# Attention on 128-pixel tiles: quarter matmuls for t, the out projection and the centring, and the q and k biases added by GpSimd

## The reference, cut to what matters

```python
xn = groupnorm(x)                       # 8 groups
t = xn @ ciw.T + cib + pe[image]        # "t"
tn = layernorm(t)
q2, k2, v2 = ((tn @ wq.T + bq) @ wiq.T + biq), ...   # q and k biases
attn = softmax(q2 . k2 / sqrt(8))       # over the 8 images, for each head
z = (attn @ v2) @ wout.T + bout         # out projection
t = z + t
tn2 = layernorm(t)                      # centring, then variance
m = (tn2 @ w1.T + b1) * gelu(t @ w2.T + b2) @ w3.T + b3
out = (m + t) @ cow.T + cob + x
```

## Time and profile before

| | us |
|---|---|
| median of 3 runs | 1245.43 |
| the profiled execution's own time | 1244.47 |
| its span, first to last instruction | 1242.5 |
| of it: before the first `pe_t` (setup) | 58.7 |
| first `pe_t` to the last `dve_x` of the attention | 627.0 |
| the rest: convolutions and the last stores | 556.8 |
| PE, DVE busy over the span | 1147.9, 1104.6 |
| ACT, POOL busy over the span | 648.7, 417.1 |

### The profile page before, as it was taken

One profiled execution on the slowest core, in us unless ns is written; L12 is line 12 of the kernel. 1 busy time (PEld: TensorE's weight loads), 2 busy tenths in 40 slices (PEclk: granted clock), 3 DMA queues, 4 the chain that ended last, 5 costly groups with the idle time before them and its releaser, 6 DMA issues. The chain is left out here.

```text
span 1242.5 us, 20220 instructions
## 1 busy us (share of the span) xinstructions
PE 1147.9 (92%) x6594; PEld 625.4 (50%) x6594; DVE 1104.6 (89%) x1521; ACT 648.7 (52%) x1518; POOL 417.1 (34%) x384
## 2 busy tenths in 40 slices
PE   3169999999999999999998899999999999999995
PEld 2156766766766776776763333333333333333331
DVE  4648999999999999999995799999999999999995
ACT  1356787787777777777763224233323422342422
POOL 3112313312322322322321344444444453455440
PEclk9989999999999999999999899999999999999998
DMA  8010111111101101101000000030001100030003
GB/s 300 18 33 18 33 29 27 35 27 29 30 25 34 25 25 34 25 25 35 18 13 14 1 1 1 1 63 5 1 1 29 40 2 1 1 68 1 1 1 68
DMA packets 87508, 35.34 MB, mean 28 GB/s; under 512 B 70209, under 2 KB 86850, under 8 KB 86930
## 3 DMA queue, kind: packets, MB, share of 16 engines
q1 hardware_dynamic: 85634, 33.81, 10.3%
q0 software_dynamic: 768, 0.33, 0.1%
q10 hardware_dynamic: 1040, 0.35, 0.1%
HBM read 26.09 MB, written 8.39 MB: 28 GB/s over the span
## 5 line engine op out<-in xcount | busy, mean ns | idle before, releaser
L1012 PE MATMUL acc<-mixed,cwp 128*128 128x512 f32 x768 | 354.8, 607 | 4.0 <-DVE mixed L1073 2.5
L1012 PEld LDWEIGHTS acc<-mixed,cwp 128*128 128x128 f32 x768 | 139.7, 191 | 217.8 <-issue 214.5
L1030 ACT ACTIVATE y<-acc,cols 128x1024 f32<-128x1024 f32 x96 | 111.8, 1210 | 249.2 <-PE acc L1022 249.2
L769 POOL TENSOR_TENSOR rstd<-var,half 128x8 f32<-128x8 f32 x32 | 80.2, 2507 | 382.0 <-DVE var L733 382.0
L1022 PE MATMUL acc<-mixed,cwp 64*64 64x512 f32 x1536 | 184.2, 600 | 11.4 <-POOL mixed L1073 11.4
L485 DVE TENSOR_TENSOR prod<-qkv 128x1024 f32<-128x1024 f32 x128 | 155.7, 1218 | 3.9 <-DVE qkv L675 1.5
L495 DVE TENSOR_TENSOR prod<-attn,qkv 128x1024 f32<-128x1024 f32 x128 | 153.2, 1216 | 0.0
L521 PE MATMUL b<-consts,prod 128*128 128x128 f32 x1024 | 139.1, 281 | 1.2 <-DVE prod L485 1.0
L1072 POOL TENSOR_TENSOR mixed<-xs 128x256 f32<-128x256 f32 x92 | 83.0, 902 | 156.7 <-DVE xs L1061 156.7
L1038 DVE TENSOR_TENSOR y<-y,acc 128x512 f32<-128x512 f32 x192 | 120.5, 679 | 15.6 <-ACT y L1030 15.6
L540 PE MATMUL b<-consts,prod 128*128 128x128 f32 x1024 | 128.8, 273 | 0.8 <-DVE var L733 0.3
(11 more groups left out here) (165 smaller groups left out, 1612.7 us busy)
## 6 DMA issues: line engine op xcount, KB each, us to landing
xs<-in_x SPq DMA_DIRECT2D x4, 2048.0 KB, 16.5
xa<-in_x SPq DMA_DIRECT2D x32, 256.0 KB, 2.7
xr<-in_x SPq DMA_DIRECT2D x64, 128.0 KB, 2.8
out_y<-xs SPq DMA_DIRECT2D x32, 256.0 KB, 4.7
cw<-in_L_conv_w POOLq DMA_DIRECT2D x2, 144.0 KB, 4.1
consts<-in_consts ACTq DMA_DIRECT2D x1, 192.0 KB
group<-in_consts SPq DMA_DIRECT2D x1, 64.0 KB
w1n<-in_L_conv_w ACTq DMA_DIRECT2D x1, 64.0 KB
```

The source lines that it names most:

```text
L1012: pe.matmul(psum[PSUM_PAIR[v, q, j]][i][:, :, :], weights(v, i, j).rearrange("p n o -> p (n o)"), mixed[v][i][:, s0:s0 + WIDE, j, :], star ...
L1030: act.activation(pairs(y[i][q][:, :, :]), m1, ACT.Identity, bias=cols[:, (6, 8)[v]:(7, 9)[v]]).then_inc(m1_out[i][q], 1)
```

## The change

- `pe_t`, `pe_z1`, `pe_center` and the `cowT` matmuls (now `pe_cow`) no longer use the block diagonal 128 x 128 matrix (or its halves in turn), but four quarter matmuls of 64 x 64, one for each quarter of the array, with half of the columns each: 8 of 128 columns for t, 4 of 256 for the out projection, 4 of 256 for the centring. The halves of the partitions now hold images 0 to 3 and 4 to 7, not the even and the odd. `pe_cow` is a step of its own behind `pe_scores_t` b = 2; its four matmuls were in two pairs.
- `pe_t` writes into `q_ps` rather than b2, and waits for `raw_out[1]`; `pe_qkv` g = 1 waits for `raw_out[0]`. `z1`, `cen2` and `sq2` are read from two banks, 256 columns of each.
- `pe_var2` takes 2 columns of `cmean` in place of 128.
- `dve_bias` becomes `pool_bias`: the same instruction on GpSimd.
- The order on all engines is written anew, over five tiles (t to t-4, 36 iterations), and no loop is left: all iterations are unrolled.

The diff, cut; of the order lists only the new ones stand. Semaphores were renamed and split to fit, and `dve_x`, `act_squares`, `act_raw` index images by d rather than e.

```diff
-            link(dve.tensor_tensor(top["tcol"][:, :], pt[0][:, 0:PAIRS], pet[:, :], ALU.add))
+            for e in range(2):
+                link(dve.tensor_tensor(top["tcol"][:, 2 * e:2 * e + 2], pt[e][:, 0:2], pet[:, 2 * e:2 * e + 2], ALU.add))
...
-                mm = pe.matmul(pt[0][half, 0:PAIRS], ciwT[half, :], gb[half, :], start=True, stop=True)
+                for k in range(2):
+                    mm = pe.matmul(pt[m][C * k:C * k + C, 0:2], ciwT[half, :], gb[half, 2 * k:2 * k + 2], start=True, stop=True)
...
-        gel = [sb(f"gel{e}", [P, N]) for e in range(2)]
-        gated = [sb(f"gated{e}", [P, N]) for e in range(2)]
+        gel = sb("gel", [P, 2 * N])
+        gated = sb("gated", [P, 2 * N])
...
+        cb = ctx.enter_context(nc.psum_tensor("cb", [P, 2, 512], F32))
+        zb = ctx.enter_context(nc.psum_tensor("zb", [P, 2, 512], F32))
...
+        b4, b2 = cb[:, 0, :], cb[:, 1, :]
+        b6, b3 = zb[:, 0, :], zb[:, 1, :]
+        HALF = N // 2
...
         def pe_t(pe, t, k):
             wait_loaded(pe, xa_in, t, k)
-            wait(pe, tn2_done, t - 3)
-            for p in range(PAIRS):
-                m = pe.matmul(b2[:, TILE * p:TILE * (p + 1)], top["resT"][:, p, :], xa[k % 2][:, p, :], start=True, stop=True)
+            wait(pe, raw_out[1], t)
+            for j in range(2):
+                for e in range(2):
+                    for d in range(2):
+                        m = pe.matmul(q_ps[half(d), e, 0, TILE * j:TILE * (j + 1)], top["resT"][half(e), 2 * d + j, half(e)],
+                                      xa[k % 2][half(e), 2 * d + j, :], start=True, stop=True)
             m.then_inc(t_mm, 1)
         def pe_qkv(pe, t, k, g):
             wait(pe, t_out, t + 1)
-            wait(pe, raw_out, 2 * t + g)
+            if g == 0:
+                wait(pe, t_out, t + 1)
+            else:
+                wait(pe, raw_out[0], t + 1)
...
         def pe_scores_t(pe, t, b):
             if b == 0:
-                wait(pe, t_out, upto(t + 2))
+                wait(pe, sq2_out, t - 1)
+                wait(pe, cen2_out, t - 1)
...
         def pe_z1(pe, t):
             wait(pe, z_out, t + 1)
+            wait(pe, shift_done, upto(t + 2))
             wait(pe, gelu_out[0], t)
-            pe.matmul(b6[:, :], top["woutT"][:, :], z[:, :], start=True, stop=True).then_inc(z1_mm, 1)
+            for e in range(2):
+                for d in range(2):
+                    m = pe.matmul(zb[half(d), e, 0:HALF], top["woutT"][half(e), half(e)],
+                                  z[half(e), HALF * d:HALF * (d + 1)], start=True, stop=True)
+            m.then_inc(z1_mm, 1)
         def pe_center(pe, t, k):
             wait(pe, z1_out, t + 1)
+            wait(pe, tn2_done, t)
             wait(pe, z_out, t + 1)
-            pe.matmul(b4[:, :], center, z1[k % 2][:, :], start=True, stop=True).then_inc(cen2_mm, 1)
+            for d in range(2):
+                for e in range(2):
+                    m = pe.matmul(cb[half(e), d, 0:HALF], center[half(d), half(d)],
+                                  z1[k % 2][half(d), HALF * e:HALF * (e + 1)], start=True, stop=True)
+            m.then_inc(cen2_mm, 1)
...
-                m = pe.matmul(b4[:, P * p:P * (p + 1)], sq2[:, TILE * p:TILE * (p + 1)], cmean, start=True, stop=True)
+                m = pe.matmul(b4[:, 2 * p:2 * p + 2], sq2[:, TILE * p:TILE * (p + 1)], cmean[:, ::C], start=True, stop=True)
...
+        def pe_out(pe, t, d):
+            for e in range(2):
+                wait(pe, gated_done[e], t + 1)
             for r in range(2):
-                pe.matmul(out_of(e, r), top["w3T"][:, :], rows(gated[e][:, :], r), start=True, stop=False)
-            for r in range(2):
-                m = pe.matmul(out_of(e, r), top["cowT"][half, :], rows(z1[k % 2][half, :], r), start=False, stop=True)
-            m.then_inc(out_mm[e], 1)
+                m = pe.matmul(out_of(d, r), top["w3T"][:, :], rows(gated[:, N * d:N * (d + 1)], r), start=True, stop=False)
+            m.then_inc(out_mm[d], 1)
+
+        def pe_cow(pe, t, k):
+            for d in range(2):
+                for r in range(2):
+                    m = pe.matmul(out_of(d, r), top["cowT"][half(d), :], rows(z1[k % 2][half(d), :], r), start=False, stop=True)
+            m.then_inc(cow_mm, 1)
...
+            for e in range(2):
+                for j in range(2):
+                    blk = 2 * e + j
+                    m = act.activation(tt[k][:, TILE * blk:TILE * (blk + 1)], q_ps[:, e, 0, TILE * j:TILE * (j + 1)],
+                                       ACT.Identity, bias=top["tcol"][:, blk:blk + 1])
...
-        def dve_bias(dve, t, k):
-            wait(dve, scaled_out, B * (t + 1))
+        def pool_bias(pool, t, k):
+            wait(pool, scaled_out, B * (t + 1))
             qk = qkv[k][:, :, 0:2 * C]
-            dve.tensor_tensor(qk, qk, top["brep"][:, :].unsqueeze(1).broadcast_to([P, B, 2 * C]), ALU.add).then_inc(biased, 1)
+            pool.tensor_tensor(qk, qk, top["brep"][:, :].unsqueeze(1).broadcast_to([P, B, 2 * C]), ALU.add).then_inc(biased, 1)
...
-            for e in range(2):
-                wait(dve, out_mm[e], t - 1)
-            dve.scalar_tensor_tensor(z1[k % 2][:, :], b6[:, :], cols[:, 1:2], tt[k][:, :], ALU.add, ALU.add).then_inc(z1_out, 1)
+            wait(dve, cow_mm, t - 1)
+            two = "p (e n) -> p e n"
+            dve.scalar_tensor_tensor(z1[k % 2][:, :].rearrange(two, e=2), zb[:, :, 0:HALF], cols[:, 1:2],
+                                     tt[k][:, :].rearrange(two, e=2), ALU.add, ALU.add).then_inc(z1_out, 1)
...
         def pe_iteration(pe, t, k, tiles):
             if tiles[0]:
                 pe_t(pe, t, k)
+            if tiles[2]:
+                pe_scores_t(pe, t - 2, 3)
+            if tiles[3]:
+                pe_av(pe, t - 3, 0)
+                pe_av(pe, t - 3, 1)
+            if tiles[2]:
+                pe_scores(pe, t - 2)
+            if tiles[3]:
+                pe_av(pe, t - 3, 2)
+            if tiles[4]:
+                pe_rstd2(pe, t - 4)
+            if tiles[3]:
+                pe_av(pe, t - 3, 3)
+            if tiles[0]:
+                pe_qkv(pe, t, k, 0)
+            if tiles[3]:
+                pe_z1(pe, t - 3)
+            if tiles[4]:
+                pe_a(pe, t - 4)
             if tiles[3]:
                 pe_center(pe, t - 3, (k - 3) % RING)
+            if tiles[0]:
+                pe_qkv(pe, t, k, 1)
+            if tiles[3]:
                 pe_g(pe, t - 3, (k - 3) % RING)
+            if tiles[4]:
+                pe_out(pe, t - 4, 0)
+                pe_out(pe, t - 4, 1)
             if tiles[1]:
                 pe_scores_t(pe, t - 1, 0)
+                pe_scores_t(pe, t - 1, 1)
             if tiles[3]:
                 pe_var2(pe, t - 3)
             if tiles[1]:
                 pe_scores_t(pe, t - 1, 2)
+            if tiles[4]:
+                pe_cow(pe, t - 4, (k - 4) % RING)
...
         def act_iteration(act, t, k, tiles):
             if tiles[1]:
+                act_squares(act, t - 1, 0)
+                act_raw(act, t - 1, (k - 1) % RING, 0)
+            if tiles[3]:
+                act_exp(act, t - 3)
+            if tiles[4]:
+                act_centered(act, t - 4)
+                act_square2(act, t - 4)
+            if tiles[1]:
+                act_squares(act, t - 1, 1)
+            if tiles[4]:
+                act_gelu(act, t - 4, 1)
+            if tiles[1]:
+                act_raw(act, t - 1, (k - 1) % RING, 1)
                 act_scale(act, t - 1, (k - 1) % RING)
             if tiles[2]:
+                act_scores_t(act, t - 2)
+            if tiles[4]:
+                act_rrep(act, t - 4)
             if tiles[0]:
                 act_t(act, t, k)
+            if tiles[4]:
+                act_gelu(act, t - 4, 0)
             if tiles[3]:
+                act_z(act, t - 3)
+
+        def dve_iteration(dve, t, k, tiles):
             if tiles[1]:
+                dve_p1(dve, t - 1, (k - 1) % RING, 1)
+            if tiles[4]:
+                dve_gated(dve, t - 4, 1)
+                dve_gated(dve, t - 4, 0)
+            if tiles[1]:
+                dve_p1(dve, t - 1, (k - 1) % RING, 2)
             if tiles[2]:
+                dve_sum(dve, t - 2)
             if tiles[0]:
                 dve_var1(dve, t)
+            if tiles[1]:
+                dve_p1(dve, t - 1, (k - 1) % RING, 3)
+            if tiles[2]:
+                dve_reciprocal(dve, t - 2)
+                dve_attn(dve, t - 2)
+                dve_p2(dve, t - 2, (k - 2) % RING, 0)
+            if tiles[3]:
+                dve_var2(dve, t - 3)
+            if tiles[2]:
+                dve_p2(dve, t - 2, (k - 2) % RING, 1)
+                dve_p2(dve, t - 2, (k - 2) % RING, 2)
+            if tiles[4]:
+                dve_x(dve, t - 4, (k - 4) % RING, 1)
             if tiles[2]:
                 dve_p2(dve, t - 2, (k - 2) % RING, 3)
             if tiles[1]:
                 dve_max(dve, t - 1)
```

(71 more changed lines are left out.)

156 lines of the change are left out of this document (37 added, 119 removed).

## The result

The changed kernel takes 1180.52 us (median of 4 runs, 1178.98 to 1180.93) against 1244.68 before: ratio 0.948, 95% interval 0.9465 to 0.9498. The profiled execution took 1180.53 us with a span of 1178.7; its outer parts moved by less than 1 us (58.6 us ahead of the first `pe_t`, 557.6 from the last `dve_x` to the end), so all of the gain lies in the attention, 562.5 us where it was 627.0.

What follows compares the result with a forecast made beforehand. TensorE was taken to bound the attention: 30 iterations falling from 18.43 to 16.8 us save 48.9 us, fill and drain add 6, so 1244.47 becomes 1201.6 profiled, 1202.5 us median; range 1188 to 1228.

Steps and rivals of the forecast that it cites:

- What bounds the kernel: Attention: TensorE sets the pace at 18.43 us per iteration; unloading only the vector engine would bring nothing.
- The quarters: TensorE's four quarter matmuls run at once: 0.58 us each for `pe_z1`, `pe_center` and `pe_cow`, 0.55 for `pe_t`.
- TensorE's sum: TensorE's work per attention iteration falls by 1.87 us, from 18.43 to 16.56 (bounds 16.0 and 17.2).
- aside on the tiling rule: TensorE's mode changes fall from 11 to 9 per iteration, which would take off another 0.2 us.
- Coupling: Waits between engines joined by single buffers add 0.25 us per attention iteration to TensorE's 16.56, giving 16.8.
- The vector engine: Without `dve_bias` (1.14 us), its need per attention iteration falls from 17.16 to 16.0 us, below TensorE's.
- GpSimd: The bias takes 2.4 us there, 7.5 us busy of 16.8; its latency costs nothing while under 3.9 us.
- cover of 1.5 us: The bias on GpSimd ends 1.5 us before its tile's first product, or 0.5 with one product colliding.
- The vector engine as the bound: Rival, chance 0.19: vector engine sets the attention's pace at 17.7 us per iteration, median 1229.5 us.
- the late bias: Rival, chance 0.05 shared with another: products hold GpSimd's bias to 6.4 us, iteration 18.8 us, median 1262.5.
- The extra tile in flight: Rival, no chance of its own: one more tile eats the gain in fill and drain; even 15 us leaves 1212.
- Quarters that don't run at once: Rival, chance 0.01: TensorE's quarter matmuls run one after another, 22.4 us per iteration, about 1370 us.

Runs made afterwards that it cites:

- b1: The kernel before with the addition of the q and k biases left out, all else as it was: 1242.79 us.
- e2: The changed kernel with the addition of the q and k biases left out on every engine: 1178.78 us.
- e9: The changed kernel with `pe_var2` in 8 matmuls of 128 x 64 instead of 4 of 128 x 128, directly behind `pe_out`: 1167.92 us.
- e3: The changed kernel with t, out projection and centring as block diagonal matmuls on the whole array again (results differ from the reference): 1224.16 us.
- e10: The changed kernel with the two halves of `pe_out` parted by the first `pe_scores_t`, adding two tiling mode changes: 1188.67 us.
- b3: The kernel before with only half the columns of `pe_t`, `pe_z1` and `pe_center` computed, on the whole array: 1230.11 us.
- e4: The changed kernel with t, out projection and centring on the whole array again and the bias back on the vector engine: 1231.49 us.
- b2: The kernel before with only the bias moved to GpSimd, in the old order: 1261.92 us.
- e1: The changed kernel with the bias back on the vector engine, just ahead of its tile's first product: 1203.54 us.
- e5: The changed kernel with the second `dve_x` moved ahead of the last `dve_p2`, which then starts after the bias: 1220.72 us.
- e6: The changed kernel with a second, unread addition of the same size on GpSimd just ahead of the bias: 1239.93 us.

## Why the prediction was wrong in size

**What bounds the kernel: right.** TensorE before and after. b1 shows that the vector engine had no share in it before, e2 that the bias on GpSimd has none after, and e9 that TensorE has it (take 0.4 us from it and the iteration falls by 0.4).

**The quarters: right, within 0.03 us each.** 0.60, 0.59 and 0.55 us for `pe_z1`, `pe_center` and `pe_t`, where 0.58, 0.58 and 0.55 were put down.

**TensorE's sum: 0.28 us too high, 16.56 for 16.28.** Three terms were mis-sized. `pe_out` was carried over at 2 x 0.59; with `cowT` parted from it, its eight instructions stand together and take 1.01: 0.16 saved that nobody had costed, though the diff shows the regrouping. `pe_cow` beside `pe_t`, both in quarters, takes 0.48 rather than 0.58, and `pe_var2` 0.81 rather than 0.89. The first two go with changes of mode that fell away: `pe_cow` takes 0.60 again in e3, ahead of a `pe_t` on the whole array, and e9 moves 0.10 out of `pe_out` in the same way. The prediction had seen that: in its aside on the tiling rule it counted 11 changes falling to 9, put 0.1 us to each and gave 0.2 us, and then left it out of the sum. By the Trainium skill's page TensorEngine Tiling (Array Packing), section Key Properties, a change of mode drains TensorE; the runs agree, and e10 puts 0.15 us on each change that it adds.

**Coupling: 0.25 us taken, nothing measured** (p is 16.28 us and TensorE's rows add up to it with no idle time). This is the step that failed in kind. It was put between two bounds by the busy shares (93% of the vector engine and no wait now; 1.27 us of idle time kept at the other end). But shares say nothing on who waits: the new order at 97% has no wait on TensorE, the old order at 95% (b3) loses 0.9 us against the busier engine, and the new order with the bias back and full matmuls (e4) loses 0.31 with the vector engine at 94%. What decides, by the waits that b2, b3 and e4 show at their handovers, is the work that stands between each result and its use, and that could have been walked through for the whole order, as it was for `pe_a` and `dve_z1`.

**Together**: 0.52 us per iteration, 15.6 us. The first and the last steps of `act_z` give 2.2 more (14.72, 15.84, 15.74 and 12.08 us where 17.60, 18.43, 17.97 and 13.04 had been), the drain 3.3: from the last `act_z` to the end of the last `dve_x` it is 17.4 us, where 19.7 had been and 20.7 were expected. The traces place 1.7 us of that between the starts of the last `pe_z1` and `pe_center` (3.38 and 1.65) and 1.2 in the last tile's `pe_out` and `pe_cow` (from 680.80 to 685.07 before, from 617.09 to 620.12 now, both at a granted clock of 0.50, 1.2 GHz). The fill was right (47.3 us from the first `pe_t` to the first `act_z`, 47.6 put down). One slip stands in the prediction's own range: p = 16.4 with 2 us of fill gives 1186.5, not 1189; the measured 1180.5 is below both.

**The vector engine: right.** The bias was put at 1.14 us and 16.0 were to be left; it needs 15.85, and with the bias back the iteration is 17.13 (e1).

**GpSimd: right in the result, wrong in the reason.** The bias takes 2.34 us alone (2.4 put down), the window is 9.94 us from `dve_var1` to the first product (10.0). But one collision was priced at 0.43 us on the vector engine and 1.0 on GpSimd, from additions of 256 elements, as if both engines shared. In the earlier trace rows the 0.43 was what was left of GpSimd's 0.61; the 1.60 in the same rows, 0.99 more than alone, was GpSimd waiting for the rest of the vector engine's addition. The price is the rest of the other's instruction: 1.1 us on GpSimd in the changed kernel, and none on its product, which keeps 1.21; on the vector engine 1.85 us in e5 and 2.15 in the fill. Of the cover of 1.5 us, 0.5 was to be left and 0.06 was: the bias took 3.43 us, as 2.4 and 1.0 have it, but started 0.35 us later than put down (6.45 us behind `dve_var1`, not 6.1). The Trainium skill (GPSIMD Engine Reference, section Specifications) names the contention, and the runs agree (3.06 us for a product of 1.22, e5).

**The rivals.** The vector engine as the bound didn't come, and neither did the late bias; both are near: e1 and e6 reach 1203.5 and 1239.9. The extra tile in flight cost 4.6 us in the fill and nothing in the drain. Quarters that don't run at once: ruled out by the sixteen instructions of `pe_t` in 0.55 us.

## What to carry to other kernels

Ask which engine is never idle, and cost its list first; then cost that list again in its new order, since 0.15 us for a change of tiling mode, times the changes, is as large as a matmul saved. Where two engines are within some per cent of each other, expect a part's worth to depend on the other part: offload and quarters gave 7 and 28 us alone, 51 together. An elementwise step on GpSimd was free here only because the order left room for its latency, and because no vector instruction with two SBUF sources started while it ran: e5 and e6 cost 40 and 59 us.

## What the runs showed of the hardware that was not expected

- The bias on GpSimd and a product on the vector engine (each with two sources in SBUF) hardly overlap: the later one does nearly all of its work behind the earlier (product 3.06 us in e5 and 3.37 in the fill of the changed kernel, instead of 1.22; bias 3.43 instead of 2.34). Instructions of the vector engine that read one source from PSUM run beside the bias at their own pace (`dve_max`, `dve_shift`, `dve_x`).
- Each added change of TensorE's tiling mode took 0.15 us (e10: 0.30 for two).
- Eight matmul instructions on the whole array take 0.81 us with 2 columns each and 0.89 with 128: the weight loads set it, which start 0.11 us apart. Sixteen on half of the array's columns take 0.51 (e9): there the loads start in pairs, some 6 ns apart, and a pair follows the last by 0.06 us, so loads into two halves go side by side.
